# Block-wise turning of every eighth probability tile in the first attention layer of a two-layer cross-attention kernel

## The reference

```python
# L0: HD = 16, KVH = 8, GROUPS = 4
q = hidden_state @ Wq + bq            # (b, 512, 512)
k = encoder_hidden_state @ Wk + bk    # (b, 1024, 128)
v = encoder_hidden_state @ Wv + bv
scores = jnp.einsum('bkgld,bksd->bkgls', q, k) * scale + mask
attn = jax.nn.softmax(scores, axis=-1)
out = jnp.einsum('bkgls,bksd->bkgld', attn, v)
out = out.transpose(0, 3, 1, 2, 4).reshape(b, l, H) @ Wo + bo
x = out + hidden_state                # then a layer norm, then the second part
```

## Time and profile before

| | |
|---|---|
| Time, median of 3 runs | 2826.98 us (2826.59 to 2828.62) |
| The profiled execution's own time | 2827.14 us |
| Its span, first to last instruction | 2825.3 us |
| Busy over the span | PE 95%, PEld 76%, DVE 61%, ACT 54%, POOL 47% |
| Granted TensorE clock, mean | 0.977 |
| Stage of the first layer, first batch | about 52 to 327 us |
| The same, second batch | about 1457 to 1731 us |

### The profile page before, as it was taken

The page is one execution under the profiler, slowest core; times in us unless marked ns, Lnnn a source line. Parts: engine busy times, 40 slices in busy tenths (PEclk is TensorE's granted clock), DMA queues, the critical chain, the costliest instruction groups (busy, mean ns, idle before and its releaser), DMA issues.

```text
span 2825.3 us, 50326 instructions
## 1 busy us (share of the span) xinstructions
PE 2680.2 (95%) x17432; PEld 2155.3 (76%) x17432; DVE 1733.9 (61%) x2626; ACT 1517.4 (54%) x2360; POOL 1323.1 (47%) x742
## 2 busy tenths in 40 slices
PE   6999979999998999997979999899999989999989
PEld 5677667888887888886856776688888778888867
DVE  5899665665555565664158996556656555656541
ACT  3888635455544455544438885454545444554443
POOL 2323235566634466654423322355665435665543
PEclk8999989999999999999989999899999999999999
DMA  8311105444521444441462110145354225354512
GB/s 203 92 32 32 62 17 130 100 119 104 131 69 54 108 112 111 124 109 55 171 134 77 39 56 31 33 114 120 99 124 112 69 54 124 97 129 106 128 47 77
DMA packets 87732, 261.94 MB, mean 93 GB/s; under 512 B 19697, under 2 KB 33281, under 8 KB 81169
## 3 DMA queue, kind: packets, MB, share of 16 engines
q1 hardware_dynamic: 87568, 259.80, 35.2%
HBM read 135.45 MB, written 6.83 MB: 50 GB/s over the span
## 4 chain that ended last, share of the span: by engine, by line
issue 39%; POOL 29%; PE 25%; DMA 2%; DVE 2%; SPq 1%; POOLq 1%; ACT 1%; DVEq 0%; ACTq 0%
POOL pT L462 16%; PE ps_t L1049 8%; POOL wa L462 5%; PE ps_m L1064 4%; POOL v L462 4%; PE ps_m L931 4%; PE ps_s L1036 3%; PE ps_s L931 3%; POOL wo L462 3%; DMA scr_q<-parts 2%; SPq L340 1%; PE ps_t L931 1%; PE ps_m L1167 1%; DMA acc<-in_rows 1%; POOL x_res L485 0%
## 5 line engine op out<-in xcount | busy, mean ns | idle before, releaser
L462 POOL TENSOR_TENSOR pT<-pT,pT 128x1024 fp32r<-128x1024 f32 x224 | 539.4, 2409 | 521.8 <-ACT pT L621 520.8
L748 ACT ACTIVATE p<-ps_s,nm 128x1024 f32<-128x1024 f32 x256 | 284.4, 1111 | 279.2 <-DVE nm L1550 279.2
L621 ACT ACTIVATE pT<-pT 128x1024 fp32r<-128x1024 f32 x224 | 237.9, 1062 | 361.1 <-DMA pT<-pb 361.1
L931 PE MATMUL ps_s<-kT,qT 128*128 128x512 f32 x1536 | 398.3, 399 | 18.1 <-ACT p L748 15.0
L1566 DVE STREAM_TRANSPOSE pb<-p 128x1024 f32<-128x1024 f32 x224 | 278.4, 1243 | 119.2 <-ACT p L748 110.5
L931 PEld LDWEIGHTS ps_s<-kT,qT 128*128 128x128 f32 x1536 | 281.0, 189 | 90.5 <-ACT p L748 29.8
L1547 DVE TENSOR_REDUCE nmx<-ps_s 128x1 f32<-128x1024 f32 x256 | 309.6, 1209 | 39.0 <-PE ps_s L931 38.8
L1475 DVE CUSTOM_DVE_ANT_0 sm<-ps_s,mask 128x1024 f32<-128x1024 f32 x256 | 309.7, 1210 | 15.5 <-PE ps_s L1036 9.2
L701 ACT ACTIVATE p<-sm,nm 128x1024 f32<-128x1024 f32 x256 | 293.5, 1146 | 44.6 <-DVE nm L1475 34.9
L1049 PEld LDWEIGHTS ps_t<-ident,p 128*128 128x128 f32 x2048 | 224.7, 143 | 103.3 <-issue 81.0
L1049 PE MATMUL ps_t<-ident,p 128*128 128x128 f32 x2048 | 287.8, 284 | 16.3 <-DVE pt L1483 9.2
(11 more groups left out here) (136 smaller groups left out, 4182.5 us busy)
## 6 DMA issues: line engine op xcount, KB each, us to landing
pT<-pb SPq DMA_DIRECT2D x896, 128.0 KB, 2.4
stg_qk<-in_wqk SPq DMA_DIRECT2D x40, 1024.0 KB, 7.4
stg_vo<-in_wo SPq DMA_DIRECT2D x48, 512.0 KB, 3.5
wob<-in_wo SPq DMA_DIRECT2D x32, 512.0 KB, 3.5
stg_vo<-in_wv SPq DMA_DIRECT2D x32, 512.0 KB, 3.7
q_stack<-scr_q SPq DMA_DIRECT2D x48, 128.0 KB, 4.4
st_ctx<-in_ctxT SPq DMA_DIRECT2D x8, 512.0 KB, 5.4
mask<-in_mask SPq DMA_DIRECT2D x2, 2048.0 KB, 12.5
```

Source lines behind the costliest of these rows:

```text
L462: return nc.gpsimd.tensor_tensor(out, x, f32(hi), ALU.subtract)
L621: return nc.scalar.activation(out, in_, ACT.Copy)
L748: nc.scalar.activation(p[t % 2][:], ps_s[t % 2][:], ACT.Exp, bias=nm[:, i:i + 1], scale=SCALE1, accum_out=sums[:, i:i + 1]).then_inc(exp_d ...
L931: mm = nc.tensor.matmul(out, lhs(x, c), rhs(y, c), start=start and c == 0 and i == 0, stop=stop and c == n_tiles - 1 and i == 2)
```

## The change

In every unit, the first step (t % 8 == 0) is no longer turned by PE. DVE turns its probabilities in 32x32 blocks into a new tile `pb0` (`blocks0`), and SyncE moves the blocks to `pt0[0]` with 16 transfers of 32 KB (`move0`). Neither the eight transposes nor the two copies of that step remain. The tile lies in `pt0[0]` in another order, so its reader takes four pieces of 32 columns. DVE's copy of step 1 goes to ACT, which makes both. The value products of the first group of a unit move from steps 5 and 7 to step 7 and step 0 of the next unit. Since `pb0` needs room, `wob` has one buffer instead of two, and SyncE interleaves its loads with the moves. The loads of the second part's first weights now stand behind all 16 moves.

```diff
@@ new tile, one buffer less
-        wob = sb("wob", [P, 2, D], F32, 2)
+        wob = sb("wob", [P, 2, D], F32)
+        pb0 = sb("pb0", [P, 4, ST * 32], F32)
@@
+        def turned_before(t):
+            return t - (t + UNIT - 1) // UNIT
+        def turned_tile0(t, st):
+            if t % UNIT == 0:
+                return pt0[t % RING][:].rearrange("p s n -> p (s n)").rearrange("p (j s n) -> p s j n", j=4, s=ST)[:, st]
+            return pt0[t % RING][:, st, :].rearrange("p (j n) -> p j n", j=4)
@@ SyncE
             def load_wob(b, f):
-                if f >= 2:
-                    sp.wait_ge(acc_done, (b * V_B + f - 1) * 2)
+                if f >= 1:
+                    sp.wait_ge(acc_done, (b * V_B + f) * 2)
                     apart()
+                def move0(u):
+                    sp.wait_ge(pb0_done, b * UNITS0 + u + 1)
+                    apart()
+                    if u >= 1:
+                        sp.wait_ge(pv0_done, b * (STEPS0 // GROUPS) + 2 * u - 1)
+                        apart()
+                    for j in range(4):
+                        for a in range(4):
+                            sp.dma_start(pt0[0][32 * a:32 * a + 32, 2 * j:2 * j + 2, :],
+                                         pb0[32 * j:32 * j + 32, a, :]).then_inc(moved0_in, 16)
@@
-                for f in range(V_B):
-                    load_wob(b, f)
+                load_wob(b, 0)
+                for u in range(UNITS0):
+                    move0(u)
+                    if u + 1 < V_B:
+                        load_wob(b, u + 1)
@@ ScalarE, exp0 and the loop over steps
-                    if t >= 2:
-                        act.wait_ge(t0_filled[1], t0 + t - 1)
+                    if t >= 2 and (t - 2) % UNIT == 0:
+                        act.wait_ge(pb0_done, b * UNITS0 + u + 1)
+                    elif t >= 2:
+                        act.wait_ge(t0_filled[1], tt0 + turned_before(t - 1))
@@
-                    copied0(t, 0)
+                    if t % UNIT > 0:
+                        copied0(t, 0)
+                    if t % UNIT == 1:
+                        copied0(t, 1)
                     if t + 2 < STEPS0:
                         exp0(t + 2)
@@ TensorE, values0 and the loop
                         for q in range(2):
-                            pe.wait_ge(t0_copied[q], t0 + t + GROUPS)
+                            pe.wait_ge(t0_copied[q], tt0 + turned_before(t + GROUPS))
+                        if e == 0:
+                            pe.wait_ge(moved0_in, 256 * (u0 + u + 1) + 16)
@@
-                turned0(0)
-                scores0(3)
-                for t in range(1, STEPS0):
-                    turned0(t)
+                for t in range(STEPS0):
+                    if t % UNIT > 0:
+                        turned0(t)
@@
-                    if t >= GROUPS and t % 2 == 1:
-                        for i in (t % GROUPS - 1, t % GROUPS):
-                            values0(t // GROUPS * GROUPS - GROUPS, i)
+                    if t % UNIT == UNIT - 1:
+                        values0(t - UNIT + 1, 0)
+                        values0(t - UNIT + 1, 1)
+                    if t >= UNIT and t % UNIT in (0, 1, 3):
+                        for i in ((0, 1) if t % UNIT == 1 else (2, 3)):
+                            values0(t // UNIT * UNIT - (UNIT if t % UNIT == 0 else GROUPS), i)
@@ VectorE
+                def blocks0(t):
+                    dve.wait_ge(moved0_in, 256 * (u0 + t // UNIT) + 16)
+                    dve.wait_ge(exp0_done, t0 + t + 1)
+                    nc.vector.transpose(pb0[:].rearrange("p a (s n) -> p s a n", s=ST),
+                                        p0[t % 2][:].rearrange("p (s a n) -> p s a n", a=4, n=32)).then_inc(pb0_done, 1)
@@
                 for t in range(2):
                     maxima0(t)
+                blocks0(0)
                 three_parts(5)
@@
-                    copied0(t, 1)
+                    if t % UNIT > 1:
+                        copied0(t, 1)
                     if t % UNIT == UNIT - 1:
                         inverse(t // UNIT)
+                        if t + 1 < STEPS0:
+                            blocks0(t + 1)
```

More of the change, by code:

```diff
@@ L45 @@
 STEPS0 = UNITS0 * UNIT
+TURNED0 = STEPS0 - UNITS0
 RING = 2 * GROUPS
@@ L226, in build @@
         t0_filled, t0_copied = [sem(f"t0_filled{q}") for q in range(2)], [sem(f"t0_copied{q}") for q in range(2)]
+        pb0_done, moved0_in = sem("pb0_done"), sem("moved0_in")
         rz0_done = sem("rz0_done")
@@ L242, in build @@
         bv_made, bv_out = sem("bv_made"), sem("bv_out")
-        acc_in, wob_in = sem("acc_in"), [sem(f"wob_in{i}") for i in range(2)]
+        acc_in, wob_in = sem("acc_in"), sem("wob_in")
         wob_scaled, acc_done = sem("wob_scaled"), sem("acc_done")
@@ L295, in load_wob @@
             def load_wob(b, f):
-                if f >= 2:
-                    sp.wait_ge(acc_done, (b * V_B + f - 1) * 2)
+                if f >= 1:
+                    sp.wait_ge(acc_done, (b * V_B + f) * 2)
                     apart()
-                sp.dma_start(wob[f % 2][:], d["wo"][f, :, :, :]).then_inc(wob_in[f % 2], 16)
+                sp.dma_start(wob[:], d["wo"][f, :, :, :]).then_inc(wob_in, 16)
             def load_qk(use, src):
@@ L429, in _ @@
                 sp.sem_inc(moved_in[j], 16)
+            sp.sem_inc(moved0_in, 16)
             load_kv(0)
@@ L508, in value_rows @@
                     y, pr = divmod(f, PAIRS)
-                    w, at_bias = wob[f % 2], (4 * y + 3) * HEADS + 2 * pr
-                    pool.wait_ge(wob_in[f % 2], 16 * (b * PAIRS + f // 2 + 1))
+                    w, at_bias = wob, (4 * y + 3) * HEADS + 2 * pr
+                    pool.wait_ge(wob_in, 16 * (b * V_B + f + 1))
                     nc.gpsimd.tensor_tensor(w[:], w[:], cols[:, at_bias:at_bias + 2].unsqueeze(2)
@@ L688, in _ @@
                     wide(2 + i, P_Q[i], cols0q[:, i:i + 1], SCALE0)
-                t0 = b * STEPS0
+                t0, tt0 = b * STEPS0, b * TURNED0
                 def exp0(t):
                     u, i = t // UNIT, t % UNIT
-                    if t >= 2:
-                        act.wait_ge(t0_filled[1], t0 + t - 1)
+                    if t >= 2 and (t - 2) % UNIT == 0:
+                        act.wait_ge(pb0_done, b * UNITS0 + u + 1)
+                    elif t >= 2:
+                        act.wait_ge(t0_filled[1], tt0 + turned_before(t - 1))
                     if t % UNIT == 0 and u >= 2:
@@ L707, in copied0 @@
                         act.wait_ge(pv0_done, b * (STEPS0 // GROUPS) + t // GROUPS - 1)
-                    act.wait_ge(t0_filled[q], t0 + t + 1)
+                    act.wait_ge(t0_filled[q], tt0 + turned_before(t + 1))
                     copy(pt0[t % RING][:, 4 * q:4 * q + 4, :], ps_t[q][:].rearrange("p (s n) -> p s n", s=4))\
@@ L1023, in _ @@
                 apart()
-                t0, u0, g0 = b * STEPS0, b * UNITS0, b * (STEPS0 // GROUPS)
+                t0, u0, tt0 = b * STEPS0, b * UNITS0, b * TURNED0
                 def place(t):
@@ L1044, in turned0 @@
                     for q in range(2):
-                        if t >= 1:
-                            pe.wait_ge(t0_copied[q], t0 + t)
+                        if t >= 2:
+                            pe.wait_ge(t0_copied[q], tt0 + turned_before(t))
                         for s in range(4):
@@ L1060, in values0 @@
                         for q in range(2):
-                            pe.wait_ge(t0_copied[q], t0 + t + GROUPS)
+                            pe.wait_ge(t0_copied[q], tt0 + turned_before(t + GROUPS))
+                        if e == 0:
+                            pe.wait_ge(moved0_in, 256 * (u0 + u + 1) + 16)
                     for st in (2 * i, 2 * i + 1):
                         for gr in range(GROUPS):
-                            mm = nc.tensor.matmul(ps_m[u % 2][gr * 2 * HD:(gr + 1) * 2 * HD, 0:P],
-                                                  v32[:, st, kv, :], pt0[(t + gr) % RING][:, st, :],
+                            mm = nc.tensor.matmul(ps_m[u % 2][gr * 2 * HD:(gr + 1) * 2 * HD, 0:P]
+                                                  .rearrange("p (j n) -> p j n", j=4),
+                                                  v32[:, st, kv, :], turned_tile0(t + gr, st),
                                                   start=e == 0 and st == 0, stop=e == 1 and st == ST - 1)
@@ L1083, in _ @@
                         scores0(t + 3)
-                    if t >= GROUPS and t % 2 == 1:
-                        for i in (t % GROUPS - 1, t % GROUPS):
-                            values0(t // GROUPS * GROUPS - GROUPS, i)
+                    if t % UNIT == UNIT - 1:
[4 more added lines that the diff above has]
+                            values0(t // UNIT * UNIT - (UNIT if t % UNIT == 0 else GROUPS), i)
+                for i in (2, 3):
+                    values0(STEPS0 - UNIT, i)
                 for i in range(4):
@@ L1465, in _ @@
                 apart()
```

(6 more changed lines are left out.)

## The result

The changed kernel takes 2852.59 us in the median of four runs (2849.26 to 2856.68), against 2827.42 for the kernel before; the ratio is 1.0089 (95% interval 1.0072 to 1.0107). It is 25 us slower, and the forecast of 2852.6 was met to the tenth. Two of its terms were off in opposite directions, one by about 10 us and one by about 6, so the closeness of the figure is luck.

The account below looks back on a forecast made before the run. PE was taken as today's bound (49.83 of 50 us busy, no holes), after the change a loop through PE, DVE and ACT. 2827.14 + 9.6 + 16 = 2852.7 us, 2852.6 on the median's scale; range 2816 to 2872.

Parts of the forecast that it names:

- the loop: Steady state: longest start-to-start chain through DVE, ACT and PE makes a unit 16.34 us instead of 16.02.
- +0.32 x 30 units = +9.6: Steady state: each unit 0.32 us longer, 9.6 us in all, the two first units reckoned apart.
- PE's waits: Steady unit: about 0.6 us ahead of step 3's turning, 0.7 ahead of the second halves of T6 and T7.
- rival 2: Steady state: DVE's load sets the pace, units stay at 16.0, only first units cost; 2843 us; chance 0.11.
- +16 for the first units: Start of each batch: PE stands until the first move lands at 88; 8 us each, 16 together (bounds 10 and 22).
- less 1 that DVE and ACT have worked ahead meanwhile: First unit of a batch: 1 us taken off for DVE and ACT working ahead during PE's stall.
- The single `wob` at no cost: SyncE's reload behind 16 issues, some 12 us into a unit, delays nobody; GpSimd's result has 16 us to spare.
- The steady move: Later units: move done at 14.1 us, products due at 15.3; hidden by 1.2 us, by nothing at worst landing.
- Rival 4: Every unit: the move is late, a 17.45 us loop, +1.43 a unit; 2886 us; chance 0.05.
- the dearer strided reading: PE's strided reading of `pt0[0]` at double price: +1 us a unit, 2883; the forecast took it at nothing.
- Rival 1: Steady state: PE stays the bound, units of 15.07 us; 2814.5 us, chance 0.11; 2798 with first units hidden, 0.05.
- The reading by occupancy: Whole stage: the engine with highest occupancy counts, DVE at 45.26 of 50, so relieving PE brings nothing.

Follow-up runs that it names:

- e2: Changed kernel with DVE's order at the unit turn: maximum 9, block transpose, maximum 10, copy 7, inverse; 2841.65 us, ratio 1.0048.
- e5: Changed kernel with the second copy of step 1 given back from ACT to DVE; 2837.53 us, ratio 1.0031.
- e4: Kernel before with only the new order of the first group's value products, no block transpose or moves; 2841.91 us, ratio 1.0046.
- e8: e7 with DVE's multiplication of a finished unit moved from step 4 to step 1 of the unit after; 2809.24 us, ratio 0.9934.
- e1: Changed kernel with step 0 of each batch's first unit turned by PE again, so without the first move; 2844.44 us, ratio 1.0054.
- e3: Changed kernel with each batch's first move issued ahead of the loads of `w0o`, `acc` and `wob`; 2857.6 us, ratio 1.0101.
- e7: Changed kernel with the edits of e1 and e2, `pb0` laid into `stg_qk` and `wob` double-buffered again; 2815.0 us, ratio 0.9950.

## Why the prediction was right

*The direction and the mechanism of the steady state held.* The prediction said that the sums of work (15.07 us on PE, 14.25 on DVE) would mislead, and that the order would give back what PE saves. The trace shows the loop link by link, e2 and e5 each took links out of it and gained 0.45 or 0.46 us a unit, down to the next longest loop, which had been put at 15.68 beforehand and measured 15.63. e4 and e8 show that second loop from both sides. Together they split a plain unit: the kernel before 16.02; the new order of the value products +0.58 (e4, 16.60); one turning less, -0.97 (e2, 15.63; the turning's distance is 0.95, and e2 differs from e4 in the work of DVE and ACT as well, so this part is a subtraction); the block transpose and the second ACT copy in the loop, +0.45 (16.08).

*The term "+0.32 x 30 units = +9.6" was too large; it measured 0.* Two steps of it failed. The loop was summed to 16.34 and is 16.08: of the 21 distances, the block transpose to maximum (1.11, not 1.17), the two from ACT's first copy of step 1 to the exponential (together 0.95, not 1.00), copy 2 to T3 (0.65, not 0.71) and R to copy 4 (1.24, not 1.29) were too long. Of the others some were a hundredth or two too long and a few too short. I had allowed for 0.1. PE's waits were too large with it: 0.37 us ahead of T3, not 0.6, and 0.17 at the second half of T6. And the unit of before was read from one unit, 16.02, though its mean over fourteen is 225.31 / 14 = 16.09, since three of the fourteen take 0.3 more. So the steady state adds nothing to the time, and all the loss that is accounted for lies at the two starts and ends of the stage. In its numbers that is rival 2, which had the unit unchanged and only the first units to pay; its reason, DVE's load, is what e2 and e5 refute.

*The term "+16 for the first units" was too small; it measured 21.6* (10.9 and 10.7 by gate to first R). The move landed at about 91, not 88: it began at 78.50, not 76.8 (the gate itself was 1.3 later), and took 12.75. The other failed step is "less 1 that DVE and ACT have worked ahead meanwhile". `blocks0` of the second unit waits until the first move has landed, for `pb0` has one buffer, and three maxima stand behind it. The profile shows DVE idle for 9.06 and ACT for 10.90. But that is not what slowed PE afterwards: up to the first R its matmul records show no wait. The slow pace behind the stall was given 1.5 us, for two pairs of quarters; it cost 2.8, since scores and a turning ran at the low clock too. Against that stands one turning less ahead of the first R, 0.95 us, which the sum for the first unit left out.

*"The single `wob` at no cost" holds in the changed kernel, but by luck.* There the first stall is so long that GpSimd's additions end (93.0 us) before the second move is due (96.16). As soon as the first stall is shortened (e1, e3), the reload stands ahead of a move that is ready, and the second unit is 6.1 to 8.5 us longer than the others. The prediction looked at who waits for `wob` and not at what is queued behind its load on SyncE.

*The steady move* was given 12.4 us from first issue to landing; it starts at 160.66 and its last issue ends at 171.34, with a median landing of 1.9 us from issue, ahead of the products due at 173.98. PE's matmuls wait for a move twice in the changed kernel, at the two first units. The margin is as thin as foretold: in e2 one move took 11.80 us to issue (219.38), and PE waited 0.20 us for it. Rival 4 falls, and with it the dearer strided reading: the quarters of a unit's first group, which read `pt0[0]`, take the same 1.08 us a pair as the others. Rival 1 falls by the unit of 16.08, and in e2 PE still waits for DVE's copies at 15.63.

*The reading by occupancy.* The Trainium skill, "Perfetto Trace Analysis", section "Identifying the Most-Contended Engine", would have optimised DVE, the engine with the highest occupancy beside PE's weight loads. It came near the truth for the steady state (a unit of 16.0) but for another reason. In e5 DVE got 0.6 us more work a unit and the unit became 0.46 us shorter; e8, the fastest version, has DVE fuller (46.09 of 50) than the kernel before (45.26).

## What to carry to other kernels

Before moving work off the engine that is the bound, add up the longest loop of starts through all engines for one period, with the order in which each stream holds its instructions; the loads of the engines only give a floor. When a transfer takes the place of engine work, look at the first period separately: there nothing has been issued ahead, sixteen issues took about 11 us here, whether of 32 KB or of 128 KB each, everything queued behind them or ahead of them in the issuing engine's queue takes part, and TensorE may come back from the stall at a lower clock. And read the period of the old kernel as a mean over many, not from one.

## What the runs showed of the hardware

- Small transfers are paced by their issue. Sixteen transfers of 32 KB took 10.0 to 12.0 us to issue, sixteen of 128 KB 10.63; a quarter of the bytes saved nothing, whether 2 MB of weights were on their way (changed kernel, 11.05) or not (e3, 10.72).
- DVE's block transpose took 1.19 to 1.25 us, about as in the second layer, also where it ran beside GpSimd's additions (1.25 us at 91.23, with additions from 90.42 to 93.03).
- Behind the long stalls of this case PE goes on at the lower clock level. It stood from 81.5 to 91.25 us in the changed kernel; the granted clock was 0.94 from 80 to 82, as it stopped, and 0.50 from 84 to 96, and a pair of quarters took 1.94 us where it takes 1.08 at 1.00. In the second batch it was 0.50 from 1508 to 1517.
- ACT hands over from a copy to the next instruction after 0.46 to 0.51 us though the copy is recorded as 0.60.
- Three in fourteen units of the kernel before take 0.3 us more. That is gone in the profiles of the changed kernel and of e7, and seen again in those of e4 (three in fourteen, up to 0.37) and e8 (two units of 15.8 where the others take 15.43). What lies behind it no row shows.
